# Scale in a register, maximum and scale on two engines, all batches written out, and rows loaded first

## The reference, cut to what matters

```python
# dense experts (every token through all 16 experts and a shared one), x is (16, 525, 192)
h = h + ffn(layernorm(h))          # routing weights w_full: softmax, groups, top 4
y = einsum('teh,ehd->td', silu(xt @ Wu + bu) * (xt @ Wg + bg) * w_full[:, :, None], Wd)

# attention, 12 heads of 16, every tensor quantised to 8 bits by its own largest value
attn = einsum('bhnd,bhmd->bhnm', fake_quant(q), fake_quant(k)) * scale
attn = softmax(attn, axis=-1)
out = einsum('bhnm,bhmd->bhnd', fake_quant(attn), fake_quant(v))
```

## Time and profile before

| | us |
|---|---|
| median of 3 runs (5014.97 to 5021.38) | 5021.34 |
| the profiled execution | 5018.49 |
| its span | 5016.8 |
| PE busy | 3730.5 (74%) |
| DVE busy | 3504.8 (70%) |
| ACT busy | 2718.9 (54%) |
| POOL busy | 1604.2 (32%) |

### The profile page before, as it was taken

One profiled execution on the slowest core, in us unless ns is written; L12 is line 12 of the kernel. 1 busy time (PEld: TensorE's weight loads), 2 busy tenths in 40 slices (PEclk: granted clock), 3 DMA queues, 4 the chain that ended last, 5 costly groups with the idle time before them and its releaser, 6 DMA issues. The chain is left out here.

```text
span 5016.8 us, 79151 instructions
## 1 busy us (share of the span) xinstructions
PE 3730.5 (74%) x23684; PEld 2834.3 (56%) x23732; DVE 3504.8 (70%) x7340; ACT 2718.9 (54%) x5075; POOL 1604.2 (32%) x1365
## 2 busy tenths in 40 slices
PE   0069999994999999999528677777677743489990
PEld 0059999993898888889514311111122223489990
DVE  7749888894666666666577599999677755645552
ACT  4535555552444444444335699999788833434430
POOL 4647777772333333334200000000000022422216
PEclk9999999996999999999755655555555555589995
DMA  3235455443222222222233700000111156233325
GB/s 99 78 104 144 130 151 140 139 138 101 75 75 75 75 75 75 75 75 73 82 100 90 248 22 21 21 21 15 62 64 64 64 170 216 89 102 114 105 88 155
DMA packets 294150, 478.09 MB, mean 95 GB/s; under 512 B 62419, under 2 KB 224187, under 8 KB 281938
## 3 DMA queue, kind: packets, MB, share of 16 engines
q1 hardware_dynamic: 274066, 448.83, 29.1%
q0 software_dynamic: 16896, 19.40, 1.4%
q10 hardware_dynamic: 2944, 6.99, 0.6%
HBM read 354.24 MB, written 123.73 MB: 95 GB/s over the span
## 5 line engine op out<-in xcount | busy, mean ns | idle before, releaser
L693 PE MATMUL b_pA<-b_woutT,b_ys 128*105 128x192 f32 x3840 | 689.6, 327 | 1.2 <-ACT b_ho L579 0.4
L976 POOL TENSOR_TENSOR c_ap<-c_ac,c_ap 128x420 fp32r<-128x420 f32 x340 | 428.2, 1259 | 772.5 <-ACT c_ap L1121 772.0
L1909 ACT ACTIVATE g_pS<-g_pS,g_stt,k_cs 128x525 f32<-128x525 f32 x816 | 627.4, 837 | 8.1 <-DVE g_junk L1936 7.5
L1936 DVE TENSOR_SCALAR_CACHE_REDUCE g_junk<-g_pS,g_csn 128x525 bf16<-128x525 f32 x816 | 606.7, 764 | 32.8 <-PE g_pS L1891 24.5
L693 PEld LDWEIGHTS b_pA<-b_woutT,b_ys 128*105 128x105 f32 x3840 | 610.8, 171 | 12.2 <-ACT b_ho L579 3.9
L1891 PE MATMUL g_pS<-g_qk 16*128 16x262 bf16 (+1 forms) x1536 | 462.2, 408 | 157.3 <-ACT g_pS L1909 141.3
L491 POOL TENSOR_TENSOR b_ys<-b_hs,b_cb 128x525 f32<-128x525 f32 x384 | 507.0, 1321 | 222.3 <-DVE b_hs L776 179.4
L1121 ACT ACTIVATE c_ap<-c_ac 128x420 fp32r<-128x420 f32 x340 | 189.2, 556 | 661.0 <-DVE c_ac L1253 659.3
L776 DVE TENSOR_TENSOR_SCAN b_hs<-b_ae,b_pB 128x525 f32<-128x525 f32 x384 | 479.1, 1248 | 39.8 <-ACT b_ae L606 5.1
L1041 PE MATMUL c_pD<-cw_wd,c_ap 128*105 128x192 f32 x4080 | 440.7, 257 | 18.5 <-POOL c_ap L976 18.5
L1041 PEld LDWEIGHTS c_pD<-cw_wd,c_ap 128*105 128x105 f32 x4080 | 426.9, 173 | 42.5 <-POOL c_ap L976 30.3
(11 more groups left out here) (384 smaller groups left out, 7977.5 us busy)
## 6 DMA issues: line engine op xcount, KB each, us to landing
b_cb<-dram_ct SPq DMA_DIRECT2D x64, 1050.0 KB, 8.3
c_wb<-dram_wt SPq DMA_DIRECT2D x60, 840.0 KB, 10.7
b_cb<-dram_ct SPq DMA_DIRECT2D x64, 525.0 KB, 7.0
c_wb<-dram_wt SPq DMA_DIRECT2D x20, 1050.0 KB
dram_qk<-f_qk SPq DMA_DIRECT2D x16, 787.5 KB, 6.0
g_qk<-dram_qk SPq DMA_DIRECT2D x16, 787.5 KB, 4.6
h_qk<-dram_qk SPq DMA_DIRECT2D x16, 787.5 KB
dram_o<-h_oT SPq DMA_DIRECT2D x16, 787.5 KB, 3.5
```

The lines of the kernel that those rows point to most:

```text
L693: ins = pe.matmul(into, ys[:, u % RING, t * TP:(t + 1) * TP], woutT[:, u % NU, :], start=(u == 0 and t % 2 == 0), stop=(u % NU == NU - 1), ...
L976: nc.gpsimd.tensor_tensor(ap[LO][:, r, :], ac[:, r, :], ap[HI][:, r, :].bitcast(F32), ALU.subtract)\
L1909: nc.scalar.activation(x, x, ACT.Exp, bias=stt[:, k, 0, c:c + 1], scale=K["cs"][:, 0:1], accum_out=stt[:, k, 1, c:c + 1]).then_inc(s["exp" ...
L1936: v.tensor_scalar(junk[:, (q + k) % 2, :], pS[:, q % RING, OFF:OFF + S], csn[:, 0:1], 3.0e38, ALU.mult, ALU.min, accum_out=stt[:, k, 0, c: ...
```

## The change

Five things are done.

1. Dense experts: SP loads the rows of chunk c+3 first in the body, not last but one.
2. Statistics pass, DVE: the multiply-and-minimum becomes a maximum with negation into a new tile `raw`. POOL multiplies that one column by the scale into `stt`, one instruction a tile, and releases ACT. POOL's products of a batch stand behind the block product of the same batch. `junk`, the negated scale and the semaphore for it go.
3. Both passes, ACT: the scale of the exponentials is read into a register once and given from there, instead of as a column of 128 equal values.
4. Statistics pass: all engines have their 16 batches written out, instead of a loop.
5. Both passes: the function table is loaded by an explicit instruction ahead of the first use; in the second pass it is a set with both logarithm and exponential.

```diff
@@ dense_experts, sync @@
             def body(c, i, k, last):
+                rows(c + 3)
                 sp.wait_ge(s_out[k], i * 16)
                 sp.dma_start(y[:, k, :, :], tiles(h1, c)).then_inc(s_y[k], 16)
                 if last < 2:
                     weights(c + 1, range(len(GROUPS)))
-                rows(c + 3)
                 store(c, k)
@@ attention_heads, first block (g_) @@
-        junk = sb("junk", [128, 2, S], BF16)
-        csn = sb("csn", [128, 1])
+        raw = sb("raw", [128, 2, NS_ + HG])
-        s = {n: sem("q_" + n) for n in ("S", "mn", "exp", "min")}
+        s = {n: sem("q_" + n) for n in ("S", "max", "mn", "exp", "min")}
@@ gpsimd @@
                 blocks(pool, qt[:, k, :, :, 0:QR], qk[:, k, 0:HG, QM:S], mask).then_inc(s_qt, 1)
 
-            two_a_turn(pool, NB, body)
+                for q in range(NQ):
+                    c = column(q)
+                    pool.wait_ge(s["max"], at(b, NQ, q + 1))
+                    if q == 0:
+                        pool.wait_ge(s_o[k], i * 144)
+                    pool.tensor_tensor(stt[:, k, 0, c:c + 1], raw[:, k, c:c + 1], K["cs"][:, 0:1],
+                                       ALU.mult).then_inc(s["mn"], 1)
+
+            pool.sem_inc(s["mn"], CREDIT)
+            written_out(NB, body)
@@ sync, tensor, scalar and vector alike @@
-            two_a_turn(pe, NB, body)
+            written_out(NB, body)
@@ scalar @@
+            cs = act.alloc_register("g_cs")
+            act.reg_load(cs, K["cs"][0:1, 0:1].bitcast(I32))
+            act.preload_act_table(ACT.Exp)
...
-                    nc.scalar.activation(x, x, ACT.Exp, bias=stt[:, k, 0, c:c + 1], scale=K["cs"][:, 0:1],
+                    nc.scalar.activation(x, x, ACT.Exp, bias=stt[:, k, 0, c:c + 1], scale=cs,
                                          accum_out=stt[:, k, 1, c:c + 1]).then_inc(s["exp"], 1)
@@ vector @@
-            v.tensor_scalar(csn[:, :], K["cs"][:, 0:1], -1.0, None, ALU.mult).then_inc(s_c, 1)
-            dve.wait_ge(s_c, 1)
...
             def body(b, i, k, last):
-                dve.wait_ge(s_o[k], i * 144)
+                dve.wait_ge(s["mn"], at(b, NQ, -NQ))
                 for q in range(NQ):
                     c = column(q)
                     dve.wait_ge(s["S"], at(b, NQ, q + 1))
-                    dve.wait_ge(s["mn"], at(b, NQ, q - 1))
-                    v.tensor_scalar(junk[:, (q + k) % 2, :], pS[:, q % RING, OFF:OFF + S], csn[:, 0:1], 3.0e38, ALU.mult,
-                                    ALU.min, accum_out=stt[:, k, 0, c:c + 1]).then_inc(s["mn"], 1)
+                    v.tensor_reduce(raw[:, k, c:c + 1], pS[:, q % RING, OFF:OFF + S], AX, ALU.max, negate=True)\
+                        .then_inc(s["max"], 1)
                     if q == 6:
                         lowest(b - 1, 1 - k)
@@ attention_heads, second block (h_), scalar @@
+            cs = act.alloc_register("h_cs")
+            act.reg_load(cs, K["cs"][0:1, 0:1].bitcast(I32))
+            act.preload_act_table_set("natural_log_exp_and_others")
...
                     nc.scalar.activation(ex[:, (n + k) % 2, :], pS[:, (n + k) % 2, :, :].rearrange("p t l -> p (t l)"),
-                                         ACT.Exp, scale=K["cs"][:, 0:1]).then_inc(s["E"], 1)
+                                         ACT.Exp, scale=cs).then_inc(s["E"], 1)
...
-                        nc.scalar.activation(exr[:, :], pR[:, 0:W], ACT.Exp, scale=K["cs"][:, 0:1]).then_inc(s["Er"], 1)
+                        nc.scalar.activation(exr[:, :], pR[:, 0:W], ACT.Exp, scale=cs).then_inc(s["Er"], 1)
```

More of the change, by code:

```diff
@@ L1816, in attention_heads @@
         pS = ctx.enter_context(nc.psum_tensor("g_pS", [128, RING, 1024], F32))
-        s_m0, s_all, s_v, s_go, s_i, s_c, s_k, s_qt = (sem(n) for n in (
-            "s_m0", "s_all", "s_v", "s_go", "s_i", "s_c", "s_k", "s_qt"))
+        s_m0, s_all, s_v, s_go, s_i, s_k, s_qt = (sem(n) for n in (
+            "s_m0", "s_all", "s_v", "s_go", "s_i", "s_k", "s_qt"))
         s_q = [sem(f"s_q{k}") for k in range(2)]
         s_o = [sem(f"s_o{k}") for k in range(2)]
-        s = {n: sem("q_" + n) for n in ("S", "mn", "exp", "min")}
+        s = {n: sem("q_" + n) for n in ("S", "max", "mn", "exp", "min")}
         block = ctx.enter_context(nc.Block())
@@ L1849, in _ @@
                 load(k, 0, k)
-            two_a_turn(sp, NB, turn)
+            written_out(NB, turn)
             for k in range(2):
@@ L1908, in body @@
                     x = pS[:, q % RING, OFF:OFF + S]
-                    nc.scalar.activation(x, x, ACT.Exp, bias=stt[:, k, 0, c:c + 1], scale=K["cs"][:, 0:1],
+                    nc.scalar.activation(x, x, ACT.Exp, bias=stt[:, k, 0, c:c + 1], scale=cs,
                                          accum_out=stt[:, k, 1, c:c + 1]).then_inc(s["exp"], 1)
-            two_a_turn(act, NB, body)
+            written_out(NB, body)
         @block.vector
         def _(dve):
-            for n in ("mn", "min"):
+            for n in ("max", "min"):
                 dve.sem_inc(s[n], CREDIT)
             dve.wait_ge(s_i, 4)
-            v.tensor_scalar(csn[:, :], K["cs"][:, 0:1], -1.0, None, ALU.mult).then_inc(s_c, 1)
-            dve.wait_ge(s_c, 1)
             def lowest(b, k):
```

2 lines of the change are left out of this document (1 added, 1 removed).

## The result

The changed kernel takes 4883.01 us, the median of 4 runs (4876.72 to 4883.32); the kernel before took 5021.36 on the same chip (5014.97 to 5021.47). The ratio is 0.9725, with an interval of 0.9708 to 0.9741. The forecast was 4881 us.

| stretch (first to last instruction named) | before, us | after, us | difference | forecast |
|---|---|---|---|---|
| dense experts, second addition into `c_y` | 1158.4 | 1117.3 | -41.1 | -40 |
| statistics pass, first to last exponential | 642.8 | 566.9 | -75.9 | -75 |
| second pass, first to last large exponential | 496.9 | 485.8 | -11.1 | -24 |
| routing to the switch experts, first to last scatter | 168.5 | 158.2 | -10.3 | 0 |
| all the rest | | | -3.4 | -1 |

The account below looks back on a forecast made before the run. ScalarE was taken to bound the statistics pass, PE most dense steps, and ScalarE only part of the second pass's chain. Savings of 40 + 75 + 25 = 140 us gave 5018.5 - 140 + 2.8 = 4881 us, range 4865 to 4905.

Parts of the forecast that it names:

- Dense rows, 40 us: Dense experts: loading rows earlier removes 17 stalls, each giving PE 2.36 us, 40 us in all.
- The register, 73 us: Statistics pass: scale from a register costs like a constant, 0.09 us less on each of 816 tiles, 73 us.
- Table load and loop, 11 us: Statistics pass: written out with one table load, six boundaries save 1.79 us each, 11 us.
- Boundaries, 6 us lost: Statistics pass: 15 batch boundaries stand 0.75 us late instead of 0.36, 6 us lost.
- The minimum at place 6: Statistics pass: DVE's two small batch-minimum instructions lose their cover, 0.2 us a batch, 3 us lost (0 to 10).
- The ring, 0.63 us a tile: Statistics pass: the PE, DVE, GpSimd, ACT turn through four PSUM slots takes 2.52 us, 0.63 a tile, below ACT's 0.68.
- the ring takes over: Rival, statistics pass: four-slot PSUM chain becomes the bound, tile about 0.73 us, gain 36 instead of 75; 4920 us, chance 0.20.
- Second pass, 25 us: Second pass: table loads save 8 us, the register 17 (55% of 30; 9 to 30), together 25.
- more than forecast: Rival: ACT bound in all of the second pass, no boundary loss; 165 us gained, 4856 us, chance 0.10.
- a register is as dear as a column: Rival, both passes' exponentials: the register scale saves nothing; 54 us gained in all, 4967 us, chance 0.08.
- the dense stall only changes its name: Rival, dense experts: DVE then waits for routing weights or su, PE gains nothing; 4921 us, chance 0.07.
- slower: Rival, statistics pass: GpSimd's product with hops costs 1.3 us a tile, 115 us net lost there; 5071 us, chance 0.03.

Follow-up runs that it names:

- g_written: The kernel before with only the statistics pass written out for all 16 batches on all five engines: 5007.68 us, ratio 0.9969.
- column_g: The changed kernel with the statistics pass's scale as a column again, all else kept: 4945.65 us, ratio 0.9854.
- hop_twice: The changed kernel with a second, unread 128x1 GpSimd product ahead of each real one in the statistics pass: 4891.95 us, ratio 0.9743.
- second_table: The kernel before with only the second pass's table load moved ahead of its loop, scale still a column: 5008.01 us, ratio 0.9982.
- second_both: The kernel before with the second pass's table load ahead of its loop and its scale from a register: 5004.57 us, ratio 0.9971.
- rows_only: The kernel before with only the load of the dense experts' rows moved to the start of SP's body: 4972.96 us, ratio 0.9904.

## Why the prediction was right, and where it was not

- **Dense rows, 40 us: 41.1.** The pair of TensorE's steps was the right measure. Taking VectorE's waits would have given 89.
- **The register, 73 us: 74.** That a register costs what a constant costs was taken without a row. No run gives the scale as a constant, but 91 ns less at 1536 columns (1542 to 1451) and 88 at 221 are near the 94 that the earlier trace rows gave for leaving a column out. In the pass, an ordinary interval fell from a mean of 0.766 us in g_written to 0.6754, and 815 x 0.0908 = 74. Against column_g it is 68.3 for the whole pass, since the boundaries and the place of the minimum are 0.09 to 0.10 us longer each with the faster exponential.
- **Table load and loop, 11 us: 10.8** by g_written.
- **Boundaries, 6 us lost: 6.** Written out, a boundary stands 0.51 us over the usual interval in g_written and 0.90 in the kernel after: 15 x 0.39 = 5.9. The step of 0.39 was right; both levels were 0.15 too low (0.36 and 0.75), because the row of 1.13 us is a boundary inside a turn of the loop, and the written-out ones take 1.27.
- **The minimum at place 6, 3 us lost: 3.** 0.19 us over the usual interval, 16 times; in g_written it is hidden altogether (0.767, the usual interval). In the kernel before it was not hidden, as the forecast had it, but stood 0.07 over the usual.
- **The pass: -74 - 10.8 + 5.9 + 3 = -75.9**, as measured.
- **The ring, 0.63 us a tile: not the bound.** The rival "the ring takes over" falls by hop_twice: even with another product in it the interval stays at 0.68. Its argument was that late exponentials are recorded longer and so free their slots late. By the intervals the records grow because ScalarE is started ahead of its own pace, and they stop growing when the slots run out.
- **Second pass, 25 us: 12. This step failed.** The table's part was 8 and measured 8.2 (6.9 in the pass and 1.3 ahead of it). The register's was 55% of 30 us, 17, and is 3.9, 13%. The step that failed is the share: I took the steps in which ScalarE shows no wait as bound by ScalarE. But the exponential hides beside TensorE's and VectorE's work there too, and making it shorter turned its time into waits (53.5 to 70.8 us by second_table and second_both). The row that should have warned was there to be asked for: by the table by stretch ScalarE was busy 429 of 497 us in the kernel before and TensorE 392 (with some 50 of its products missing from that trace), and TensorE waited 38.5 us for VectorE's copy. An engine that is idle in 14% of a stage, and waits 57 times, gives no share of its time by counting the other steps.
- **The stage nobody touched, 0: -10.3.** The forecast said "more instructions to fetch", at nothing. It was neither nothing nor a loss: the changed kernel has 117 packets of 8 KB in the one instruction queue instead of 138, and 115 of 16 KB in the other instead of 106, so about as many bytes in all (2.84 and 2.87 MB), and its routing loop lost 8.8 us of idles.

So the 140 us of the sum are right by two errors that cancel: 13 us too many in the second pass, 10 too few in a stage without an edit. The other terms are 1 us off each, and 2 us are elsewhere. For the dense rows, the statistics pass and the table loads the mechanism was right as well as the sum; that 4881 is within 2 us of 4883 is chance. Two rivals' sums are slightly off as written: the ring's comes to 37 us and not 36, "more than forecast" to 162 and not 165; neither changes a verdict. Of the rivals, "a register is as dear as a column" fell to every exponential's record, "the dense stall only changes its name" to rows_only, and "slower" to the product's 191 ns. "The ring takes over" fell to hop_twice, and "ACT bound in all of the second pass" was the far side of the very term that failed.

The Trainium skill (GPSIMD Engine Reference, 4.1 Engine selection) advises against such work on GpSimd. No run compares the two engines on one product. For products of one column on GpSimd the runs show no harm: 191 ns each, and the pass is 4.7 us shorter than with VectorE's combined operation, which had become the slowest link.

## What to carry to other kernels

An operand moved from an SBUF column to a register took about 0.09 us off each of ScalarE's exponentials here, but only the stage where ScalarE has no idle bracket turned that into time: ask which engine the others wait for, and do not count the steps without a wait. To price a removed stall, take the pace of the engine that ends the stage, with and without it (7.5 against 9.9 us), never the waits of the engine that stood. After each edit compare the stages that were not edited as well: in this kernel a stage that nobody edited moves by 3 to 11 us with edits elsewhere, more than several of the edits are worth.

## What the runs showed of the hardware

- A scale from a register instead of an SBUF column makes ScalarE's exponential 91 ns shorter at 128x1536 (1542 to 1451 ns), 88 at 128x221 (445 to 357), and lets one of 128x525 follow every 0.675 us instead of 0.766.
- ScalarE takes a new exponential of 525 columns with accumulation every 0.674 us; the record of each then grows, from 0.67 to 0.88 us within 40 tiles (from 0.76 to 0.94 over a batch with the column), and from there it takes one every 0.680. From place 10 on, start and record together give an end every 0.68 us. So a growing record is read here as work started ahead of its pace, not as contention.
- VectorE's 128x525 maximum from PSUM follows at 0.61 us when nothing holds it (by GpSimd's products behind it, 2991.55 to 2992.16 in hop_twice), as from SBUF. Its multiply-and-minimum takes 0.69.
- A product of 128x1 on GpSimd takes 191 ns, and two in a row start 0.14 to 0.15 us apart.
- Idles of 2.1 to 2.6 us with "issue" as their cause, in front of an instruction in a loop when the loop comes round, go with a packet of 8 KB in a queue of kind "instruction" in the same 2 us: each of the four in the kernel before has one.
